# A decoder layer on one core: the last mixer rounds in an order of their own

## The reference

```
x = x + attention(layernorm(x))                 # 16 heads of 32, causal
x = x + mixer(ctx, ctx, layernorm(x), kernel, D, head_dim=8)
x = x + ffn(layernorm(x))

mixer:  kv[i,j,h,l] = k[i,h,l] * v[j,h,l];  y = causal convolution of kv with kernel[h] over l, plus D[h]*kv
        out[j,h,l] = sum_i y[i,j,h,l] * q[i,h,l]        # 32 heads, l = 0..511
ffn:    xq = round-trip of x through 8 bits, one scale per token;  w1, w2 the same, one scale per row
        h = silu(xq @ w_gate.T) * (xq @ w_up.T)         # width 1408
        hq = round-trip of h, scale = max(|h|)/127 per token
        return hq @ w2q.T
```

## Time and profile before

| | |
|---|---|
| median of 3 runs | 1252.67 us (1250.62 to 1254.04) |
| profiled execution, its own time | 1247.43 us |
| its span, first to last instruction | 1245.6 us |
| TensorE busy / VectorE / GpSimd / ScalarE | 92% / 81% / 77% / 71% of the span |
| mean granted TensorE clock | 0.962 of full |
| one full round near the end (from one `y_out` to the next, 1181.0 to 1196.97) | 16.0 us |
| after the last convolution (ends at 1199.7 us) | 46 us, for three heads' remaining work |

### The profile page before, as it was taken

One profiled execution on the slowest core, in us unless ns is written; L12 is line 12 of the kernel. 1 busy time (PEld: TensorE's weight loads), 2 busy tenths in 40 slices (PEclk: granted clock), 3 DMA queues, 4 the chain that ended last, 5 costly groups with the idle time before them and its releaser, 6 DMA issues. The chain is left out here.

```text
span 1245.6 us, 33765 instructions
## 1 busy us (share of the span) xinstructions
PE 1140.4 (92%) x10142; PEld 815.2 (65%) x10142; DVE 1004.4 (81%) x3161; ACT 882.4 (71%) x1819; POOL 963.4 (77%) x1113
## 2 busy tenths in 40 slices
PE   7889999999999999997676999999999999999985
PEld 5677777777777777775344566666666666666642
DVE  5678888878788887887496888898888898888872
ACT  4778888878787888888382566666766666766663
POOL 1378777767777777787644999999999999999971
PEclk9989999999999999998767999999999999999996
DMA  6447654556556455555473433444433444433400
GB/s 205 103 162 228 223 162 150 185 165 190 188 177 192 150 168 179 171 173 179 148 268 110 135 100 131 131 143 143 131 111 128 132 143 142 131 114 124 125 27 25
DMA packets 87840, 186.57 MB, mean 150 GB/s; under 512 B 12176, under 2 KB 28816, under 8 KB 87760
## 3 DMA queue, kind: packets, MB, share of 16 engines
q1 hardware_dynamic: 86896, 185.02, 47.3%
q10 hardware_dynamic: 864, 0.66, 0.3%
HBM read 105.86 MB, written 54.61 MB: 129 GB/s over the span
## 5 line engine op out<-in xcount | busy, mean ns | idle before, releaser
L649 ACT ACTIVATE prob<-masked,negmax 128x128 f32<-128x128 f32 (+1 forms) x512 | 206.3, 454 | 67.0 <-DVE negmax L777 66.1
L777 DVE CUSTOM_DVE_ANT_0 masked<-s_ps,mask_f 128x128 f32<-128x128 f32 (+1 forms) x512 | 161.1, 352 | 31.0 <-PE s_ps L530 18.3
L1022 PE MATMUL y_ps<-kv,toep 128*128 128x288 f16 x640 | 184.7, 289 | 1.4 <-DVE prod L1358 1.4
L1023 PE MATMUL y_ps<-kv,toep 128*128 128x288 f16 x640 | 184.4, 288 | 0.0
L1024 PE MATMUL y_ps<-kv,toep 128*128 128x288 f16 x640 | 184.3, 288 | 0.0
L1078 PE MATMUL f_ps<-w1T,xiT 128*128 128x512 bf16 (+1 forms) x768 | 174.8, 364 | 0.9 <-ACT xiT L1199 0.7
L1206 ACT ACTIVATE silu<-gate,sx 128x512 f32<-128x512 f32 (+1 forms) x96 | 66.0, 688 | 139.5 <-DVE gate L1412 139.5
L1257 POOL TENSOR_TENSOR tree<-prod 128x512 f32<-128x512 f32 x128 | 163.1, 1274 | 1.2 <-DVE prod L1358 1.2
L409 POOL TENSOR_TENSOR kv_s<-kv_f,kv_s 128x1152 f16<-128x1152 f32 x64 | 152.4, 2381 | 0.6 <-ACT kv_s L663 0.6
L783 DVE TENSOR_TENSOR pT_lo<-t_ps,pT_hi 128x384 f16<-128x384 f32 x256 | 140.8, 550 | 11.1 <-ACT pT_hi L657 10.5
L402 POOL TENSOR_TENSOR kv_f<-c_in 128x1024 f32<-128x1024 f32 x64 | 146.0, 2281 | 0.2 <-issue 0.2
(11 more groups left out here) (159 smaller groups left out, 3500.0 us busy)
## 6 DMA issues: line engine op xcount, KB each, us to landing
kv_pairs<-kv_s SPq DMA_DIRECT2D x64, 576.0 KB, 3.3
kv<-kv_pairs SPq DMA_DIRECT2D x32, 1152.0 KB, 8.0
c_in<-in_ctxr SPq DMA_DIRECT2D x64, 192.0 KB, 2.5
x_in<-in_x SPq DMA_DIRECT2D x16, 512.0 KB, 6.3
q_st<-q_hi SPq DMA_DIRECT2D x128, 64.0 KB, 2.0
k_st<-k_hi SPq DMA_DIRECT2D x128, 64.0 KB, 2.0
x_res<-in_x SPq DMA_DIRECT2D x16, 512.0 KB, 5.7
x_after_attention<-x_out SPq DMA_DIRECT2D x16, 512.0 KB, 4.2
```

The costliest lines, as they stand in the source:

```text
L649: ins = nc.scalar.activation(prob[h % 2][:, at:at + w], masked[h % 2][:, at:at + w], ACT.Exp, bias=negmax[:, h % 2, t:t + 1], scale=-1.0)
L777: ins = nc.vector.tensor_tensor_reduce(masked[h % 2][:, at:at + w], s_ps[h % 2][:, at:at + w], mask_f[:, S - w:S], -1.0, FAR, ALU.add, ALU ...
L1022: nc.tensor.matmul(dst, toep[p][:, 0, taps], c[:, 0, m], start=mt == 0, stop=False)
L1023: nc.tensor.matmul(dst, toep[p][:, 0, taps], c[:, 1, m], start=False, stop=False)
```

## The change

Rounds 33 and 34 are taken out of `rounds` on all engines and written out, and head 31's work gets another order:

- TensorE: all six gate and up products of head 31 first, back to back in program order; then for head 30 and for head 31 the transposes, followed by the down product. The transposes of head 30 wait for the last `ups_scaled` of head 31 (they use `f_ps[1]`); the up product of head 31 waits only for head 29's copy out of `f_ps[1]`.
- ScalarE: `silus(31, 0)` and `silus(31, 1)` stand inside the rounding of head 30, `silus(31, 2)` behind it, ahead of the two `hidden_out` copies of head 30. For head 31 ScalarE only does the three `scaled` steps; there is no `hold` for head 31.
- VectorE: the three `whole` steps of head 31 (new, `tensor_scalar` with one constant). `down_scaled(30)` moves from between `hidden_max(31, 0)` and `gates_scaled(31, 2)` to behind these. `down_scaled(31)` writes to the buffer of `x_t`, and `last_out` adds `x2[1]` to it on VectorE into the buffer of `x_q`.
- GpSimd: the three `hiddens(31, c)`, then `outs(30)`; no `outs(31)`.
- SyncE: the stores of head 31 come from `last_y`, after `last_done`.
- `sh` becomes two tiles, one per parity of the head, because head 31's scale is made before head 30's down product has been scaled.

```diff
-    hmax, sh = sb("hmax", [P, 1], F32), sb("sh", [P, 1], F32)
+    hmax, sh = sb("hmax", [P, 1], F32), [sb(f"sh{p}", [P, 1], F32) for p in range(2)]
...
+    last_down, last_y = x_t, x_q
+    last_done = sem("last_done")
...
-        for r in range(NH - 2, NH + 3):
+        for r in range(NH - 2, NH + 1):
...
             rounds(sp, body)
+            body(NH + 1, 1)
+            sp.wait_ge(last_done, 1)
+            for half in range(2):
+                sp.dma_start(tokens(out, NH - 1, half), last_y[half * 64:half * 64 + 64, :]).then_inc(out_stored, 16)
...
                 if part == 0:
+                    if isinstance(h, int) and h == NH - 2:
+                        pe.wait_ge(up_done, NH * 3)
...
-                        reached(pe, hiT_done, h * 2 - 1)
+                        reached(pe, hiT_done, h * 2 - 1 if not (isinstance(h, int) and h == NH - 1) else h * 2 - 3)
...
             rounds(pe, body)
+            for c in range(len(CH)):
+                gate_up(NH - 1, c)
+            for h in (NH - 2, NH - 1):
+                hidden_turned(h, 0)
+                hidden_turned(h, 1)
+                project_down(h, 0)
+                project_down(h, 1)
...
+                if isinstance(h, int) and h == NH - 1:
+                    for c in range(len(CH)):
+                        scaled(c)
+                    return
                 scaled(0)
                 scaled(1)
                 whole(0)
+                if isinstance(h, int) and h == NH - 2:
+                    silus(NH - 1, 1, 0)
                 scaled(2)
                 whole(1)
+                if isinstance(h, int) and h == NH - 2:
+                    silus(NH - 1, 1, 1)
                 whole(2)
...
             rounds(act, body)
+            silus(NH - 1, 1, 2)
+            hidden_out(NH - 2, 0)
+            hidden_out(NH - 2, 1)
+            round_hidden(NH - 1)
+            hidden_out(NH - 1, 0)
+            hidden_out(NH - 1, 1)
...
             rounds(pool, body)
+            for c in range(len(CH)):
+                hiddens(NH - 1, c)
+            outs(NH - 2)
...
+            def last_out():
+                dve.wait_ge(down_done, NH)
+                nc.vector.tensor_tensor(last_y[:], last_down[:], x2[1][:], ALU.add).then_inc(last_done, 1)
+
+            def whole(h, c):
+                at, w = CH[c]
+                dve.wait_ge(ht_done, h * 3 + c + 1)
+                dve.wait_ge(hi_full, h * 2)
+                nc.vector.tensor_scalar(hid_i[:, at:at + w], hid_t[:, at:at + w], MAGIC, None, ALU.subtract).then_inc(hi_done, 1)
...
             rounds(dve, body)
+            for c in range(len(CH)):
+                gates_scaled(NH - 1, c)
+                ups_scaled(NH - 1, c)
+                if c > 0:
+                    hidden_max(NH - 1, c - 1)
+            hidden_max(NH - 1, 2)
+            hidden_scale(NH - 1, 1)
+            for c in range(len(CH)):
+                whole(NH - 1, c)
+            down_scaled(NH - 2, 0, down)
+            down_scaled(NH - 1, 1, last_down)
+            last_out()
```

More of the change, by code:

```diff
@@ L1370, in hidden_scale @@
                 dve.wait_ge(hmax_done, h + 1)
-                nc.vector.tensor_scalar(sh[:], hmax[:], sx[p][:, 0:1], QMAX * EPS_Q, ALU.mult, ALU.max).then_inc(sh_done, 1)
+                nc.vector.tensor_scalar(sh[p][:], hmax[:], sx[p][:, 0:1], QMAX * EPS_Q, ALU.mult, ALU.max).then_inc(sh_done, 1)
                 dve.wait_ge(sh_done, h + 1)
-                nc.vector.reciprocal(sh_rec[:], sh[:]).then_inc(shr_done, 1)
+                nc.vector.reciprocal(sh_rec[:], sh[p][:]).then_inc(shr_done, 1)
                 dve.wait_ge(shr_done, h + 1)
@@ L1399, in token_scale, with down_scaled @@
                 nc.vector.tensor_scalar(x_mul[:], rstd3[:], v_rec[:, 0:1], -QMAX, ALU.mult, ALU.mult).then_inc(xmul_done, 1)
-            def down_scaled(h):
+            def down_scaled(h, p, to):
                 dve.wait_ge(d_full, h + 1)
-                reached(dve, out_done, h)
-                nc.vector.scalar_tensor_tensor(out=down[:], in0=a_ps[:], scalar=sh[:, 0:1], in1=s2_b[:],
+                reached(dve, out_done, min(h, NH - 1) if isinstance(h, int) else h)
+                nc.vector.scalar_tensor_tensor(out=to[:], in0=a_ps[:], scalar=sh[p][:, 0:1], in1=s2_b[:],
                                                op0=ALU.mult, op1=ALU.mult).then_inc(down_done, 1)
+            def last_out():
[6 more added lines that the diff above has]
+                nc.vector.tensor_scalar(hid_i[:, at:at + w], hid_t[:, at:at + w], MAGIC, None, ALU.subtract).then_inc(hi_done, 1)
             def gates_scaled(h, c):
@@ L1452, in body @@
                 if live(r - 3, loop):
-                    down_scaled(r - 3)
+                    down_scaled(r - 3, 1 - p, down)
                 if live(r - 1, loop):
```

## The result

| | before | after |
|---|---|---|
| median of the runs compared | 1252.04 us (6 runs, 1247.51 to 1254.04) | 1238.48 us (6 runs, 1235.84 to 1243.32) |
| ratio | | 0.9899 (95% interval 0.9866 to 0.9932) |
| profiled execution, its own time | 1247.43 us | 1243.32 us |
| its span | 1245.6 us | 1241.5 us |

The change makes the kernel faster: 13.6 us by the medians, 8.5 to 16.8 by the interval. In a second session, with more runs of before, it was 10.4 us (0.9921, 0.9900 to 0.9942). The forecast of 1243.8 us had the sign right and the size too small, and 1238.48 lies under its range of 1240.5 to 1249.0.

What follows compares the result with a forecast made beforehand. The prediction took one chain of waits at the end, with a falling clock, as the cost; TensorE paces full rounds. Gains 5.6 + 1.0 + 1.7 + 0.6 = 8.9 us took 1252.67 to 1243.8 us, range 1240.5 to 1249.0.

Steps and rivals of the forecast that it cites:

- What bounds the end: Last 16 us: no engine is short; one chain of waits, its last hidden piece late through up 0, plus low clock.
- Part 1: Head 31's gate and up products go first: last hidden piece starts at 1222.1 instead of 1227.79; gain 5.6 us.
- rival (a): Clock never falls in the new order, every matmul at 2.4 GHz: gain 11.1, 1241.6 us; chance 0.15.
- a clock partly low: Main forecast: clock falls at 1215.7, returns about 1219.1 in head 31's products; 1243.8 us, own range 1242 to 1247; chance 0.62.
- What was queued behind: Head 30's delayed rounding, transposes and scaling of its down product, behind head 31's work, were to cost nothing.
- Part 2: Head 31's rounding shared between ScalarE and VectorE: 2.3 us instead of 3.28, gain 1.0 (0.7 to 1.1).
- Part 3: Head 31's transposes and down product: 4.4 us instead of 6.06, gain 1.7 (0 to 2.3).
- Part 4: Head 31's output add on VectorE instead of GpSimd: gain 0.6 us; stores unchanged at 3.78 us.
- (b): Clock stays at 1.2 GHz from 1215.7 to the end: gain 3.9, 1248.8 us; chance 0.14.
- (c): Head 31's six products come no earlier, VectorE emptying banks no faster: gain 1.6, 1251.1 us; chance 0.05.
- (d): Second `sh` tile shifts later tiles and slows all 32 rounds; at 0.4 us a round, 1256.6 us; chance 0.04.

Runs made afterwards that it cites:

- order_only: The changed kernel, but ScalarE alone rounds head 31 and GpSimd adds its output after a hold; ratio to the kernel before 0.9941.
- tail_split: The changed kernel with gate 2 read earlier, second copy shared, down product in column halves, last stores issued by SyncE and ScalarE; ratio to before 0.9897.
- before_again: The kernel before, run again with no edit; ratio 1.0002 to the kernel before.
- pe_gap: The changed kernel, but TensorE waits after gate 0 of head 31 until ScalarE has scaled head 30's last piece; ratio to before 0.9952.

## Why the prediction was wrong in size

- **What bounds the end.** Right: a chain of waits, its late link the up side of head 31, and the clock on top.
- **Part 1, the products.** 5.6 us forecast, 7.2 measured (14.54 - 7.31). The step that failed is the one marked as a choice: I let the clock fall at 1215.7 as in before. In the four traces of after it stayed at 2.4 GHz until behind the last product. The durations of the ledger hold: with the clock high, 7.25 (rival (a): 1220.5) and 7.31 measured. With it low, 8.85 worked out and 8.90 measured in order_only, but so close by luck: there the clock fell 0.4 us earlier than I had it, gate 1 was read 0.4 us later (6.17 against 5.75), and only the later steps agree.
- **What the choice of the clock got wrong.** I gave a clock partly low 0.62 and rival (a) 0.15. The record has the clock held in four of four traces of after and fallen in both unfilled traces with the same products (order_only, tail_split), so the fall that I forecast does occur, and what decides between the two stays open. The pause behind gate 0, which the change removes, goes with a longer low stretch (6.7 against 3.3 us); that it causes the fall is not shown.
- **What was queued behind.** Right: ScalarE's silus inside head 30's rounding, the late transposes of head 30 and the late `down_scaled(30)` cost nothing. TensorE's 1.21 us in front of head 31's transposes ends on the rounding, not on head 30's down product.
- **Part 2, the rounding.** 2.3 us forecast; 1230.17 to 1232.40, so 2.2. VectorE's pieces took 0.428 and 0.360 us, against 0.43 and 0.37 by the slope and 0.36 by the estimate from the Trainium skill (VectorE: DVE Perf Modes: two elements a cycle from the perf-mode tier table, the fixed cost from the section on the TRN2 errata). This trace agrees with that estimate: 0.360 us.
- **Part 3, transposes and down product.** 4.4 taken between 3.8 and 6.1; measured 1232.46 to 1236.25, so 3.8: the gain was 2.3, not 1.7. I had taken a part of the last matmuls as slow, and the clock held.
- **Part 4, output.** 0.6 forecast, 0.63 measured (0.04 + 0.69 against 1.35); the stores 3.74 against 3.78.
- **Sum.** 7.2 + 1.0 + 2.3 + 0.6 = 11.1, the number of rival (a), to which I had given 0.15. The range ended at (a) less 1 us of scatter, and (a) with 11.1 us is itself some 2.4 us short of the 13.6 measured; no tail accounts for that rest. But the part ahead of the tail alone moves by up to 7 us between executions, so medians of a few runs differ by 2 us and more; the low end had to be nearer to 1239. Of the 5.3 us between 1243.8 and 1238.48, 2.2 are the clock (1.6 in part 1, 0.6 in part 3) and 0.1 the other parts, 2.4 I put down to scatter, and 0.6 come from the median of before, 1252.67 in three runs and 1252.04 in six.
- **Rivals (b), (c), (d).** (b), the clock low through to the end, in no trace; order_only came nearest, with two falls. (c) fell: the products came 7.2 us earlier. (d) fell: full rounds are the same to 0.03 us of busy time on VectorE and GpSimd, and after's rounds from first to last convolution take 532.9 against 532.3 us, where (d) asked for 9 or more.

## What to carry to other kernels

Where a chain of short TensorE bursts ends a kernel, price it twice, with every burst at 2.4 and at 1.2 GHz, and give both times: here the same edit was worth 5.2 us by order, 4.3 by the clock and 1.6 by shared work, and the clock's part was the one forecast badly. A wait put into such a chain can cost more than its length (2.04 us cost 4.6 in one trace with the clock low, 2.2 with it held). Filling TensorE's idle stretches with matmuls nobody reads is the cheap test of how much of a tail is the clock. Cut two traces at an event that the change does not move before comparing their spans: 4.1 us between spans hid 11.2 us of gain.

## What the runs showed of the hardware

- The same program of TensorE, up to the last up product of head 31, ran at 2.4 GHz in four traces (after) and fell to 1.2 GHz within these products in two (order_only, tail_split), with the same 2.4 us of idle time ahead of the token transposes.
- Once fallen there, the clock was low for some 3.3 us where TensorE went on working (order_only, tail_split) and for some 6.7 us where it stood for 2 us behind gate 0 (before, before_again, pe_gap).
- In tail_split a store of half a tile issued by ScalarE showed 1.43 us on its queue, SyncE's beside it 0.60, and the end of the span came 0.4 us later than with both from SyncE.
- Untouched code ahead of the tail took 1213.3 to 1220.4 us (before, after) from one execution to the next, most of it before the first convolution (666.8 to 673.3 us).
